# The tower of a feature-crossing model in chunks of four units, its sums turned into rows through memory, and the last units spread in parts

## The reference

```python
e = stack([tbl_f[ids[:, f]] for f in range(16)], axis=1)      # [512, 16, 256]
xk = e
for i in range(3):
    z = einsum('bfe,bge->bfge', e, xk).reshape(512, 256, 256)
    z = relu(einsum('bcl,oc->bol', swapaxes(z, 1, 2), Ws[i]) + bs[i][None, :, None])
    z = sum(z, axis=-1)                                       # [512, 16]
    outs.append(z)
    xk = broadcast_to(z[:, :, None], (512, 16, 256))
h = concatenate([concatenate(outs, 1), dense_ctx], axis=1)    # [512, 64]
h = maximum(h @ W_top1 + b_top1, 0)                           # 512 wide
h = maximum(h @ W_top2 + b_top2, 0)                           # 256 wide
y = h @ W_top3
```

## Time and profile before

| | us |
|---|---|
| median of 3 runs | 171.51 (171.51 to 172.08) |
| the profiled execution | 171.46 |
| its span, first to last instruction | 169.6 |
| granted clock of TensorE, mean | 0.99 |
| busy: PE / DVE / ACT / POOL | 137.1 / 144.9 / 126.3 / 121.0 |

### The profile page before, as it was taken

The page is one execution under the profiler, slowest core; times in us unless marked ns, Lnnn a source line. Parts: engine busy times, 40 slices in busy tenths (PEclk is TensorE's granted clock), DMA queues, the critical chain, the costliest instruction groups (busy, mean ns, idle before and its releaser), DMA issues.

```text
span 169.6 us, 6453 instructions
## 1 busy us (share of the span) xinstructions
PE 137.1 (81%) x2728; PEld 92.4 (54%) x2728; DVE 144.9 (85%) x136; ACT 126.3 (74%) x441; POOL 121.0 (71%) x84
## 2 busy tenths in 40 slices
PE   0045998988887878787879797999898999993995
PEld 0024665746464646464646464757474876763963
DVE  3169986999999999999999999999999998198330
ACT  3020465586979797979797979798999998977461
POOL 1777989898888888888888888989797995000000
PEclk9999999999999999999999999999999999999599
DMA  2343653131313030303030303031313100000000
GB/s 56 94 123 97 190 151 97 30 98 37 93 33 95 25 101 12 112 9 117 2 114 10 103 20 103 24 99 35 96 32 97 31 4 4 6 0 2 4 0 0
DMA packets 5273, 9.98 MB, mean 59 GB/s; under 512 B 2179, under 2 KB 2947, under 8 KB 5252
## 3 DMA queue, kind: packets, MB, share of 16 engines
q0 software_dynamic: 3072, 8.39, 17.2%
q1 hardware_dynamic: 2036, 1.29, 2.8%
q10 hardware_dynamic: 144, 0.00, 0.0%
HBM read 9.68 MB, written 0.00 MB: 57 GB/s over the span
## 4 chain that ended last, share of the span: by engine, by line
PE 46%; DVE 19%; ACT 18%; issue 8%; POOL 4%; DMA 3%; DVEq 1%; ACTq 0%
PE Y L627 25%; DVE PR L311 13%; ACT prod L387 8%; ACT XT L357 7%; PE T L592 5%; POOL X L329 4%; PE T L688 4%; PE ZB L648 4%; DVE prod L503 3%; PE Y L633 2%; ACT Y L378 2%; PE YD L670 2%; DMA X<-in_table,idx 2%; PE YD L688 2%; PE YD L604 1%
## 5 line engine op out<-in xcount | busy, mean ns | idle before, releaser
L311 DVE TENSOR_TENSOR PR<-T,XT 128x1024 f32<-128x1024 f32 (+2 forms) x72 | 101.1, 1450 | 7.0 <-ACT XT L357 6.9
L627 PE MATMUL Y<-PR,w_sb 128*32 128x272 f32 x1024 | 66.0, 399 | 13.0 <-DVE PR L311 12.6
L329 POOL DMA_INDIRECT X<-in_table,idx x64 | 61.2, 956 | 20.7 <-issue 16.1
L387 ACT ACTIVATE prod<-prod,bias_sb 128x256 f32<-128x256 f32 x122 | 60.1, 498 | 4.2 <-DVE prod L503 4.2
L311 POOL TENSOR_TENSOR PR<-XT 128x2048 f32<-128x2048 f32 (+2 forms) x16 | 59.7, 3734 | 0.3
L627 PEld LDWEIGHTS Y<-PR,w_sb 128*32 128x32 f32 x1024 | 31.1, 110 | 35.7 <-issue 12.1
L503 DVE TENSOR_TENSOR prod<-U,ZB 128x2048 f32<-128x2048 f32 (+1 forms) x18 | 35.6, 1982 | 3.4 <-PE ZB L648 3.3
L378 ACT ACTIVATE Y<-Y,bias 128x136 f32<-128x136 f32 x64 | 21.5, 336 | 14.2 <-PE Y L633 14.2
L592 PE MATMUL T<-ident_sb,X 128*128 128x128 f32 x128 | 21.7, 314 | 12.3 <-DMA X<-in_table,idx 12.3
L357 ACT ACTIVATE XT<-T 128x1024 f32<-128x1024 f32 (+1 forms) x17 | 16.6, 974 | 18.1 <-PE T L592 13.2
L592 PEld LDWEIGHTS T<-ident_sb,X 128*128 128x128 f32 x128 | 17.5, 211 | 14.0 <-issue 9.9
(11 more groups left out here) (48 smaller groups left out, 69.3 us busy)
## 6 DMA issues: line engine op xcount, KB each, us to landing
X<-in_table,idx POOLq DMA_INDIRECT x64, 2.8
w_sb<-in_w SPq DMA_DIRECT2D x1, 512.0 KB
w_sb<-in_w SPq DMA_DIRECT2D x1, 224.0 KB
sel_sb<-in_sel SPq DMA_DIRECT2D x1, 128.0 KB
ident_sb<-in_ident SPq DMA_DIRECT2D x1, 64.0 KB, 2.1
w1l_sb<-in_w1l SPq DMA_DIRECT2D x1, 64.0 KB
w2l_sb<-in_w2l SPq DMA_DIRECT2D x1, 64.0 KB
w_sb<-in_w SPq DMA_DIRECT2D x1, 64.0 KB
```

Source lines behind the costliest of these rows:

```text
L311: return eng.tensor_tensor(pr, x0.broadcast_to(shape), x1.broadcast_to(shape), ALU.mult)
L329: pool.indirect_dma_start(out=X[:, n % NV, g, :], out_offset=None, in_=table, in_offset=bass.IndirectOffsetOnAxis(ap=idx[:, NT * n + g:NT ...
L387: last = act.activation(q, q, ACT.Relu, bias=bias_sb[:, l + 1:l + 2], accum_out=to)
L627: pe.matmul(Y[TR * j:TR * j + TR, h, 0:YC], w0_sb[:, c, :], PR[:, v, h, c, CB * j:CB * (j + 1), :].rearrange("q b s -> q (b s)"), start=c ...
```

## The change

- The tower goes in four chunks of four units (128 samples). The ids are permuted on the host so that a chunk's samples stand in the order of its columns.
- The sums of a chunk are turned into rows of `H` by SP: for each layer one transfer writes them to a tensor in memory (`sums_rows`) and a second one reads them back (`to_rows`). Only layer 2 of chunk 2 and layers 1 and 2 of chunk 3 still use `select` on PE. `H` has one more row, of ones, which carries the bias of the first tower layer; `H` is zeroed once by VectorE.
- Chunks 0 and 1 run in steps 7 to 14 (`TOWER_LOOP`), a part a step: part 0 waits for the rows (`h_in`) and does the first half of the hidden layer 1, part 1 the second half, parts 2 and 3 a half of hidden layer 2 each, part 3 the output too. PE waits for ScalarE's copies there. Chunks 2 and 3 run in the end part. The last chunk's second layer is computed with the samples on partitions, and VectorE makes the output by one weighted sum (`weighted`, `y_last`), stored by a second transfer of 128 x 1.
- PE's step becomes `contract(n-1, 0)`, `spread_rows(n-2)`, `transpose(n+1)`, tower, `contract(n-1, 1)`, tower, `layer_u(n)`; ScalarE's `fill(n+1)` stands ahead of `square(n)` and `sum_y(n-1, 1)`.
- GpSimd's share begins with unit 2 (`POOL_FIRST`), with four units gathered before it; it is 4 rows, 5 for units 9 and 14, and 8 for unit 15. Unit 1 is all VectorE's.
- `prod` has three buffers. Stages 14 to 16 are spread in parts (`PIECES`), two of them between the products of the last contractions. Two halves, (13, 1) and (14, 1), are summed by folding on GpSimd and one reduction on VectorE; other sums are split anew (`ACT_SHARE`, `ACT_SUMS`).
- PE runs 10, 8 and 7 products that nobody reads (`keep_busy`) in the first steps.

```diff
-POOL_ROWS = {0: 0, NU - 2: 6, NU - 1: 6}
-TAIL_SHARE = {(NU - 2, 0): 2, (NU - 1, 0): 2, (NU, 1): 2}
+POOL_FIRST = 2
+POOL_ROWS = {9: 5, 14: 5, NU - 1: 8}
+ACT_SHARE = {(NU - 2, 0): 2, (NU - 1, 1): 2, (NU, 1): 2, (NU - 3, 1): 0, (NU - 2, 1): 0}
+FOLDS = [(NU - 3, 1), (NU - 2, 1)]
+PIECES = [(NU - 2, 0), (NU - 2, 1), (NU - 1, 0), (NU - 1, 1), (NU, None)]
+PIECE_BLOCKS = [(0, SB), (SB, 2 * SB), (0, CB), (CB, 2 * SB), (SB, 2 * SB)]
...
+            def to_rows(k, l, landed):
+                sp.dma_start(rows[k, l].rearrange("p (n b) -> p n b", b=SB), sums_of(k)[l])\
+                    .then_inc(sums_out[k], 16)
+                sp.wait_ge(sums_out[k], 16 * (l + 1))
+                sp.dma_start(H[TR * l:TR * l + F, PW * k:PW * (k + 1)].rearrange("q (g i) -> q g i", g=P // F),
+                             rows[k, l].rearrange("(g q) i -> q g i", q=F)).then_inc(landed, 16)
+            for k in range(NK):
+                sp.wait_ge(z0_ready, 2 * PC * (k + 1))
+                to_rows(k, 0, h_in if k < LAST else h_last_in)
+                if k < LAST:
+                    wait_sums(sp, (PC * (k + 1) - 1, 0))
+                    to_rows(k, 1, h_in)
+                if k < FLOW:
+                    wait_sums(sp, (PC * (k + 1), 1))
+                    to_rows(k, 2, h_in)
...
+            pool.wait_ge(bias_in, 16)
+            for s, l in FOLDS:
...
+                if (s, l) == FOLDS[0]:
+                    pool.wait_ge(prod_ready, outer_done((s, l)))
+                    pool.tensor_scalar(q, q, bias_sb[:, l + 1:l + 2], 0.0, ALU.add, ALU.max)\
...
+                pool.tensor_tensor(q[:, :, 0:P], q[:, :, 0:P], q[:, :, P:2 * P], ALU.add)\
...
+                pool.tensor_tensor(q[:, :, 0:P // 2], q[:, :, 0:P // 2], q[:, :, P // 2:P], ALU.add)\
+                    .then_inc(folded, 1)
...
+            sum_prod((NU - 4, 1), [0])
+            square(NU - 1)
+            read_behind(NU - 2)
+            read_u(NU - 2)
+            read_u(NU - 1, (0,))
+            sum_y(NU - 2, 0)
+            sum_prod((NU - 4, 1), [1])
+            sum_prod((NU - 3, 0), [0])
+            sum_y(NU - 2, 1)
+            sum_prod((NU - 3, 0), [1, 2, 3])
+            sum_prod((NU - 4, 1), [2])
             sum_y(NU - 1, 0)
-            sum_prod(NU - 2, 0)
+            sum_prod((NU - 2, 0))
+            sum_prod((NU - 4, 1), [3])
             sum_y(NU - 1, 1)
+            read_u(NU - 1, (1,))
+            relu_prod((NU - 2, 1))
+            read_selected(LAST - 1, 2)
+            sum_prod((NU - 1, 0))
+            read_hidden1(LAST - 1, 0)
+            read_hidden1(LAST - 1, 1)
+            sum_prod((NU - 1, 1))
+            sum_prod((NU, 1))
...
+            outer(NU - 2, [0], 0)
+            spread_z(NU - 2, 1)
+            spread_z(NU - 1, 0)
+            outer(NU - 2, [1], 1)
+            sum_prod((NU - 2, 0))
+            spread_z(NU - 1, 1)
+            outer(NU - 1, [0], 0)
+            outer(NU - 1, [0], 1)
+            outer(NU - 1, [1], 1)
+            sum_fold((NU - 3, 1))
             spread_z(NU)
+            sum_prod((NU - 1, 1))
             outer(NU, [1])
+            sum_fold((NU - 2, 1))
+            sum_prod((NU, 1))
...
+            def step(n, v, r, k=None, part=None):
+                contract(n - 1, 1 - v, 0)
...
+                spread_rows(n - 2)
+                transpose(n + 1, 1 - v, r + v)
...
+                if part == 1:
+                    pe.wait_ge(h1_ready, 2 * k + 1)
+                    first_hidden(k, 1)
+                elif part in (2, 3):
+                    pe.wait_ge(h1_ready, 2 * k + 2)
...
+                    second_hidden(k, part - 2)
+                contract(n - 1, 1 - v, 1)
+                if part == 0:
...
+                    pe.wait_ge(h_in, 16 * 3 * (k + 1))
+                    pe.wait_ge(u_read, n)
+                    first_hidden(k, 0)
...
+                elif part == 3:
+                    pe.wait_ge(h2_ready, 2 * k + 2)
+                    outputs(k)
+                layer_u(n, v)
...
+            layer_u(NU - 1, last, (0,))
+            contract(NU - 2, 1 - last, 0)
+            spread_rows(NU - 3)
+            contract(NU - 2, 1 - last, 1)
+            contract(NU - 1, last, 0, [(NU - 2, 0)])
+            contract(NU - 1, last, 1, [(NU - 2, 1), (NU - 1, 0)])
+            layer_u(NU - 1, last, (1,))
+            select(LAST - 1, 2)
+            spread_rows(NU - 1, 1)
...
+                first_hidden(LAST - 1, half)
             spread_rows(NU)
...
+            second_hidden(LAST - 1, 0)
+            second_hidden(LAST - 1, 1)
```

More of the change, by code:

```diff
@@ L19 @@
 NV = 2
+NPR = 3
 EH = 64
@@ L427, in _ @@
-            read_u(NU - 1)
-            for piece in MLP_STEPS[NU - 1]:
-                evacuate(piece)
+                if n == 1:
+                    fill(2)
+                for half in STAGES:
+                    if half[0] == n - 2 and half != (NU - 4, 1):
+                        sum_prod(half)
+            sum_prod((NU - 4, 1), [0])
[5 more added lines that the diff above has]
+            sum_prod((NU - 4, 1), [1])
@@ new lines, in first_hidden, with second_hidden @@
+            def first_hidden(k, half):
+                w = k if isinstance(k, int) else 0
+                for c in range(2):
+                    at = (2 * half + c) * P
+                    last = pe.matmul(hidden1_psum(w, half)[:, c, :], w1_sb[:, at:at + P], H[:, columns(k)],
+                                     start=True, stop=True)
+                last.then_inc(hidden1, 1)
+            def second_hidden(k, c):
+                w = k if isinstance(k, int) else 0
+                for q in range(HC1):
+                    last = pe.matmul(hidden2_psum(w, c), w2_sb[:, q, c * P:(c + 1) * P], h1_of(w, q),
+                                     start=q == 0, stop=q == HC1 - 1)
+                last.then_inc(hidden2, 1)
@@ new lines, in outputs, with keep_busy @@
+            def outputs(k):
+                w = k if isinstance(k, int) else 0
+                for q in range(HC2):
+                    last = pe.matmul(output_psum(w), w3_sb[:, q:q + 1], h2[:, q, :], start=q == 0,
+                                     stop=q == HC2 - 1)
+                last.then_inc(output, 1)
+            def keep_busy(to, count):
+                for _ in range(count):
+                    pe.matmul(to, ident_sb[:], ident_sb[:], start=True, stop=True)
+            pe.wait_ge(ident_in, 16)
@@ L736, in _ @@
-            contract(NU - 1, last, 1)
-            for done in MLP_STEPS[NU - 1]:
-                wait_sbuf(pe, done)
-            pe.wait_ge(u_read, NU)
-            for c in range(HC1):
-                tower((1, HIDDEN1, c))
-            spread_rows(NU - 1)
-            n0 = CHUNKS[2][0]
-            select(2, 0, n0, NU)
-            select(2, 1, n0, NU - 1)
-            select(2, 2, n0, NU - 2)
-            tower((1, HIDDEN2, 0))
-            spread_rows(NU)
-            tower((1, HIDDEN2, 1))
@@ L750, in _ @@
-            select(2, 1, NU - 1, NU)
-            select(2, 2, NU - 2, NU).then_inc(mlp_psum[2], 1)
-            for c in range(HC1):
-                tower((2, HIDDEN1, c))
-            tower((1, OUTPUT, 0))
-            for c in range(HC2):
-                tower((2, HIDDEN2, c))
-            wait_sbuf(pe, (1, OUTPUT, 0))
-            tower((2, OUTPUT, 0))
+            contract(0, 0, 0)
+            layer_u(0, 0)
+            contract(0, 0, 1)
+            transpose(2, 0, 1)
+            layer_u(1, 1)
@@ new lines, in _ @@
+            pe.wait_ge(z0_ready, 2)
+            keep_busy(Y[:, 1, 0:P], 7)
+            for n in range(2, LOOP[0]):
+                step(n, n % NV, n // NV)
+            with nc.tensor.Fori(1, len(LOOP) // NV + 1) as i:
+                step(NV * i + 1, 1, i)
+                step(NV * i + 2, 0, i + 1)
+            with nc.tensor.Fori(0, len(TOWER_LOOP) // PC) as i:
+                for part in range(PC):
+                    n = FIRST + part
+                    step(PC * i + n, n % NV, PC // NV * i + n // NV, i, part)
@@ new lines, in _ @@
+            pe.wait_ge(y_done, LAST - 1)
+            pe.wait_ge(u_read, NU)
+            for half in range(2):
+                first_hidden(LAST - 1, half)
+            spread_rows(NU)
+            pe.wait_ge(h1_ready, 2 * LAST)
+            second_hidden(LAST - 1, 0)
+            second_hidden(LAST - 1, 1)
+            pe.wait_ge(minus_half_ready, 2)
+            pe.matmul(last_psum, ones[:], b2row_sb[:], start=True, stop=False)
+            select(LAST, 1)
+            select(LAST, 2)
+            pe.wait_ge(h_last_in, 16)
@@ new lines, in _ @@
+            pe.wait_ge(h_ready, 3)
+            for half in range(2):
+                first_hidden(LAST, half)
+            for q in range(HC1):
+                if q < 2:
+                    pe.wait_ge(h1_ready, 2 * LAST + 1 + q)
+                else:
+                    pe.wait_ge(h1_dve, q - 1)
+                tile = pe.matmul(last_psum, h1_of(LAST, q), w2_sb[:, q, :], start=False, stop=q == HC1 - 1)
```

(3 more changed lines are left out.)

589 lines of the change are left out of this document (295 added, 294 removed).

## The result

The changed kernel takes 174.37 us, the median of 4 runs (173.84 to 176.33), beside 171.8 us of the kernel before, taken with it (171.51 to 172.1). The ratio is 1.017, 95% interval 1.010 to 1.024: it is slower, by 1.7%, where 163.9 us and a gain were forecast. The profiled execution took 176.33 us, with a span of 174.5; the others had spans of 171.9 to 173.1. The forecast span was 162.0, so 12.5 us have to be found in the profiled execution, the slowest of the four; between the medians it is 10.5 (174.37 against 163.9).

The account below looks back on a forecast made before the run. VectorE bounds the middle, GpSimd just behind; TensorE's queue and a relay bound the end. The hand sum of 160.8 plus 0.3 for transfers and 0.9 for hand-offs gives span 162.0, plus 1.9 time 163.9 us; range 161.2 to 168.5.

Parts of the forecast that it names:

- Steady steps: Units 3 to 13: nothing gained; VectorE keeps 8.52 us a step, GpSimd 8.64.
- The start: First units: 0 to -0.45 us; VectorE starts 0.45 earlier, GpSimd starts unit 2 at about 24.0 instead of 27.45.
- GpSimd's lead: From unit 2 on: GpSimd 3.45 us earlier, less 0.93 for unit 9, leaving 2.5 for unit 15's gathers and last products.
- the drift: GpSimd's 0.12 us a step, with unit 9's 0.93, uses up the cover; PE waits up to 1 us at units 12 to 14.
- the saved 3.1 us: Last contraction: contract(15,1) ends at 146.8 instead of 149.9.
- The transfers: Tower chunks at units 7 and 11: PE waits for sums written and read back; +0 to +1 us, 0.3 taken.
- rival (c): Units 7 and 11: transfers of 12 us a pair hold up every engine, time put at 175 us; chance 0.06.
- The end part: From the last contraction (146.8) to the weighted sum (159.2): 12.4 us and 0.9 of hand-offs, 13.3.
- Rival (a): End part: TensorE's clock falls to 1.2 GHz, +1.9 us, time 165.8; chance 0.17.
- The store: End of the kernel: 128 pieces of 4 bytes take 1.6 us as now, with 0 to +0.7 for the pieces.

Follow-up runs that it names:

- h1_norows: f3_turned_warm without the two transfers a layer for chunks 0 and 1, whose tower reads what stands in `H`: 167.7 us, ratio to the kernel before 0.973.
- h2_delayed: f3_turned_warm with the first transfer of chunks 0, 1 and 2 held until unit 4k+6 is transposed: 167.38 us, ratio to the kernel before 0.971.
- h3_pitch: The changed kernel with the last sums stored 512 bytes apart in another array, left out of the output: 169.98 us, ratio to the kernel before 0.985.
- f2_turned: The changed kernel with the last sums turned into a row by a matmul and stored with the rest: 169.03 us, ratio to the kernel before 0.982.
- f3_turned_warm: f2_turned plus nine unread matmuls in TensorE's idle time in the end part: 167.94 us, ratio to the kernel before 0.977.

## Why the prediction was wrong, step by step

**Steady steps: right as far as VectorE went.** It is busy for 17.00 of 17.00 us at 60 to 77. GpSimd's period is 8.67 to 8.68, not 8.64: over twelve periods 0.4.

**The start: half right.** VectorE starts at 9.75 instead of 9.96 and needs no more than before. GpSimd's 24.0 was wrong, and this is the step that failed first. The working put `XT` of unit 2 at 24.0; but TensorE transposed the second half at 23.90 only, having waited 1.37 us for unit 2's last gather, issued at 18.00, while SP's loads of the tower's weights (17.2 to 25.7) ran. `XT` was there at 25.9. I had asked when the gathers are issued, and not what shares the DMA engines with them; that the weights are the cause is argued from this overlap, not shown.

**GpSimd's lead, and with it the last contraction.** 1.9 of the later start, 0.4 of the period and 0.06 of the row make 2.36 us at unit 14 (130.96 against 128.6). The forecast for contraction(14,0) was 136.5; it began at 139.71. From there to the end of the last one the working had 10.3 us and the trace has 10.4, so four half-contractions and their hand-offs were right and only their start wasn't. The prediction knew the drift and priced it as up to 1 us of TensorE's waits at units 12 to 14; it did not follow it on, to gathers that stand behind GpSimd's own product, and transposes that now stand ahead of a contraction. h1_norows shows that chain to unit 14, h2_delayed to unit 15. In the changed kernel itself the chain leaves GpSimd at 90.9, by the hole of unit 10, and goes on through TensorE, ScalarE and VectorE and a read back of sums at 110.6; there the two paths are about equally late, for without the hole (h3_pitch) the end is the same. In the kernels with the new order, where the kernel before takes 171.6 to 171.8 us, the time from GpSimd's product of unit 14 to the end of the last contraction is 19.0 to 20.1 us, before it was 18.9 (131.14 to 150.0); the two of 20.1 are h1_norows and h2_delayed, whose clock fell in that stretch for 1.6 us. f2_turned begins at 25.67 and ends at 150.3, f3_turned_warm at 26.70 and 151.2; but h1_norows begins at 25.57 and ends at 150.8, so the start alone doesn't set the end. That the saved 3.1 us went to GpSimd is therefore a reading of the chain and of this count, and not shown by an experiment: the edit that would move its cadence alone ran only in the slow groups, and the low clock behind a late gather and the writes of chunk 2 beside the gathers are in the same 3 us.

**The transfers: the wait that was priced is small, the one that wasn't is the hole.** TensorE's waits for `H` come to 0.8 us. But the first transfer of a layer, in its DMA group (size, median us from issue to landing), is slow by its pieces:

```profile
H<-sums_rows SPq DMA_DIRECT2D x9, 8.0 KB, 1.7
sums_rows<-zz SPq DMA_DIRECT2D x7, 8.0 KB, 3.4
sums_rows<-z SPq DMA_DIRECT2D x2, 8.0 KB, 1.4
```

The same 8 KB take 3.4 us as 512 pieces of 16 bytes and 1.4 as 128 of 64. I had 2.2 and up to 1 for the first, 5 for a pair; at unit 7's end it took 3.9 to the second's issue and 1.7 more, 5.6. The Trainium skill gives a fixed cost of about 2.0 us in "DMA: Bandwidth & Descriptors", Anatomy of one DMA, a section on transfers issued by GpSimd. These are issued by SP; the second transfer (1.7) is near that figure, the first (3.4) is not. During that write a gather took 5.24, and one beside the first chunk's write (issued at 49.93) 4.71. Without the write, in h1_norows, the same gather, issued at 85.32, was there when TensorE took it at 88.71, 3.4 later. The hole of 2.95 and 0.58 it made is real, yet taking it away (h1_norows, h2_delayed) brought no time that the intervals can tell, for VectorE was ahead of GpSimd by then and met the next wait at unit 14, where a write of chunk 2 stood beside the gather and the clock fell once more. The end of rival (c) did not come; its place, TensorE's queue at parts 0, was the wrong one; the transfers were felt in the gathers' landing.

**The end part: the size right but for the clock, in part by luck.** With store and clock mended, f3_turned_warm has 12.9 us from the last contraction (151.21) to the turn of the last sums (164.09), against 13.3 of the working. One term was missing, though: between the last spread and `select` TensorE has the 16 tower matmuls of chunk 2 and its bias, 2.05 + 0.62 us in f3_turned_warm, and the chain goes through them. The working had an outer product and sums there, 2.6 us, which run beside them; that the two are equally long is luck. In the changed kernel the end part is 16.15. Rival (a) had the mechanism and 1.9 for it; in the profiled run two stretches at a low clock (1.2 GHz in the second) cost 3.67 - 2.05 and 3.60 - 1.91, 3.3 together. And (a) looked only at the end: the clock fell in the steps as well, behind late gathers, for 1.3 us at unit 10 and for 1.6 in three of the experiments (f3_turned_warm, h1_norows, h2_delayed). How cold the end runs differs between executions: f2_turned's had one of the two. I had given it 0.17 since the idle stretch, 150.1 to 151.5, seemed short; the clock fell nevertheless. The first operation of the fold took 3.70 us on GpSimd, not 1.9 at most; its sums were ready at 151.2 all the same, 2.8 before VectorE read them at 153.93.

**The store: the term that decided, 6.65 of the 12.5 us.** It had 1.6 with 0 to +0.7 for the pieces; it measured 8.25. The upper bound was taken from a 64 KB load and nothing in the rows had 4-byte pieces, so the bound was no bound: an operation the trace doesn't show was given a range of 0.7 us. The Trainium skill, in "DMA: Bandwidth & Descriptors", Why small descriptors are slow (HBM only), charges each piece a few cycles and some metadata; by that the spread-out pieces of h3_pitch should cost as much as neighbouring ones, and they took 1.1 against 6.8, so what is slow here is something that section doesn't state.

## What to carry to other kernels

Before a result is stored from one column of 128 partitions, turn it to a row: 0.7 us of matmul and copy took the wait from 6.8 to 0.9 us, and nothing stands behind a last store to hide it. When an engine is given a head start, follow it to the last consumer: a lead of GpSimd is spent by whatever delays its first unit, and its gathers carry that delay to TensorE's queue. And a hole that an experiment closes without the time changing is not yet a cause; look for the chain that takes its place, and read the granted clock in each hole, since the work behind a wait may be slower than the same work elsewhere.

## What the runs showed of the hardware

- 128 neighbouring pieces of 4 bytes: 6.8 us of wait; 512 bytes apart: 1.1; one piece for the whole output: 0.9.
- Writing 8 KB to memory: 3.4 us in 16-byte pieces, 1.4 in 64-byte ones; a gather beside the first landed in 5.24 us, the same one without it in 3.4 (h1_norows).
- TensorE's granted clock fell behind waits for a gather in the middle of the kernel: the engine was busy for 0.39 of the 2 us at 88 to 90 and was granted 0.57 in 90 to 94; the transposes, tower piece and contraction behind such waits took 4.90 to 5.23 us instead of 3.61.
- GpSimd: a two-step operation with a per-partition scalar took 3.70 us for 1024 elements, 3.6 ns each; the sum of two operands 1.27 for 512, 2.5 ns each, and the product 3.71 for 2048, 1.8 ns each.
- The kernel before takes 171.6 us in some groups of runs and 205 to 209 in others, where TensorE waits for the issue of its instructions. The record gives chip 0 for a group of either kind, so whether it is the chip or something of the moment isn't shown. An experiment about cadence says little in the second kind, and the kernel before says which kind it is.
